# Moving a head's weight maxima and scaling between phases of a gated delta-net block on Trainium2

## The chip, the core and the metric

The kernel runs on one core of one Trainium2 chip. The core has five engines that run their own instruction streams and meet at semaphores: TensorE (PE, matrix products), VectorE (DVE), ScalarE (ACT), GpSimd (POOL) and SyncE (SP, which here only issues transfers). Transfers between the chip's memory and the engines' memory go through queues that an engine fills: SyncE, ScalarE and GpSimd each have one here. The metric is the device time of one launch in microseconds (us), the median of several runs.

## The reference

The block adds half a feed-forward branch, an attention branch and half a feed-forward branch again, each behind a layer norm, to x of 4 x 512 tokens by 512 features. The weights of the feed-forward branch (2048 inner features) are rebuilt from spline control points. The attention branch is a gated delta rule, a recurrence over tokens with a 128 x 128 state for each of 32 value heads, two to each of the 16 key heads.

```python
x = x + 0.5 * ffn(layernorm(x)); x = x + attn(layernorm(x)); x = x + 0.5 * ffn(layernorm(x))
# attn: qkvz = x @ W_qkvz (512 x 12288, 768 columns a key head); ba = x @ W_ba (512 x 64)
# q, k, v: causal convolution of 4 taps, silu; q, k: rms norm
# beta = sigmoid(b);  g = -exp(A_log) * softplus(a + dt_bias)
def step(Sst, inp):
    q_t, k_t, v_t, g_t, beta_t = inp
    Sst = Sst * jnp.exp(g_t)[..., None, None]
    kv = jnp.einsum('bhk,bhkv->bhv', k_t, Sst)
    delta = (v_t - kv) * beta_t[..., None]
    Sst = Sst + k_t[..., None] * delta[:, :, None, :]
    o = jnp.einsum('bhk,bhkv->bhv', q_t, Sst)
    return (Sst, o)
# out: rms_norm(o) * norm_w * silu(z) @ W_out
```

## The kernel before

The program is a row of phases, one behind the other: the spline phase (to about 60 us of the profiled span) rebuilds the feed-forward weights, `ffn_phase` "f1_" is the first feed-forward block (to 343), `norm_phase` (to 422) makes the second layer norm and the gates of all heads, `attn_phase` (to 3450) is the attention, and `ffn_phase` "f2_" (to the end) the second feed-forward block. Each engine has one stream of instructions per phase, in the order in which the code writes it, and instructions of one engine run in that order.

**Weights of the attention.** Products of this phase are made from 16-bit pairs. A weight is loaded as 32-bit numbers (`raw_w`, three parts of 128 x 1024 for keys and queries, values, and Z; `raw_o` for the output weight), scaled by a power of two that puts its largest entry in a fixed place, and then cast to a high and a low half on GpSimd (`split_part`, L2341 and L2342; `split_wo`, L2352 and L2353). To find the power of two, VectorE takes a maximum along each partition (`largest`, L2209), SyncE writes these to the chip's memory and reads them back to all partitions (`most_dram`, `spread`), and VectorE takes the maximum across (`power_of_two`, L1082 to L1084), makes a table of scales (`head_scales`, L1089 to L1092) and multiplies (`scale_weights`, L2228). The result's scale is undone by the table at L2202.

**The attention phase** runs 64 units j, four batches for each of 16 key heads (j // 4 is the head, j % 4 the batch). A unit first goes through the inverse steps s = 2 to 13, in which TensorE and VectorE build a triangular inverse (TensorE L1854 and L1856; VectorE's masked product L2268; ScalarE's copy L2048), with pieces of other work written between them by a dictionary `steps[s]`. Then comes the chunk phase, c = 0 to 3: the state is carried through four chunks of 128 tokens. VectorE copies or updates the state at the head of each chunk (L2286 for c = 0, L2288 for c = 1 and 2). Preparation of the next unit and output of the last one run between.

Of the next head's weights, unit 1 of a head has the maxima at steps 4, 9, 10 and 13, unit 2 the scales at step 4 and the scalings at steps 9, 9, 10 and 11:

```python
                if has_delta and j // B + 1 < NK:
                    if j % B == 1:
                        for i, s in enumerate((4, 9, 10, 13)):
                            steps[s].append(lambda i=i: largest(i))
                    if j % B == 2:
                        steps[4].append(next_scales)
                        for part, s in enumerate((9, 9, 10, 11)):
                            steps[s].append(lambda part=part: scale_weights(part))
```

GpSimd casts the new weights in units 2 and 3. SyncE's stream for a head is: decays of the next unit (`at_gb`, L1562), taps and gates of the next head (L1097 to L1099, L1568), the rows of the residual out and in (L1579, L1574), the raw parts (L1554) and the raw output weight (L1609), and later the round trip of the maxima.

**The norm phase** goes through 16 chunks of 128 tokens: statistics on VectorE (`stats`), a power on GpSimd, a scaling on ScalarE (L1326), a turn on TensorE (L1410), halves of the result on ScalarE and VectorE. The gate weights `w_ba` make a round trip of their own (maximum behind chunk 3, scales behind chunk 6 at L1082, scaling and halves on GpSimd behind chunk 7, L1231), and TensorE's first product with them, `gates_of(0)`, is L1385. The first head's raw weights are loaded (L1191), their maxima taken behind the last chunks (L1279), and the round trip ends between the two halves of the gates' work on VectorE (L1292 to L1301). The last thing of the phase is the turn of the decays on TensorE (L1416), for which L1306 on VectorE is needed.

**The first feed-forward block** starts with x turned for the first tile of 512 tokens and then runs 4 tiles t of 16 cells n. In each cell TensorE makes two products, ScalarE the SiLU (L791) and the high half (L797), VectorE the rest. Before it, on SyncE's queue, the weights are written to the chip's memory for the second block (L711, the dump: `ffn_weights<-ffn_w`).

## Time and profile before

| | |
|---|---|
| median of 3 runs | 3742.67 us (3741.57 to 3743.55) |
| the profiled execution | 3737.42 us |
| its span | 3735.7 us |
| TensorE's mean granted clock | 0.977 |

The span is the time from the first to the last instruction of the profiled execution, and all starts below count from its beginning. The profile gives the busy time of each engine (PE, DVE, ACT, POOL; PEld is TensorE's loading of weights), the order of each engine's instructions with start, length and form, and in brackets how long the engine had been idle before one and what ended that. "x3" behind a row says that three like instructions in a row are drawn together, and their time is from the start of the first to the end of the last. SPq and ACTq are issues of transfers by SyncE and ScalarE.

### The profile page before, as it was taken

Reading aid. Unit: us, or ns where it says so; the run is one execution under the profiler, and the core shown is the slowest. Engines: PE = TensorE matmul, PEld = TensorE weight load, DVE = VectorE, ACT = ScalarE, POOL = GpSimd, SP = SyncE. Lnnn points to the kernel's source line nnn. Section 1 sums busy time; section 2 is a strip of 40 time slices with the busy share of each in tenths; the row PEclk is TensorE's granted clock in tenths of the full one; section 3 lists DMA queues with packets and bytes.
Section 4 is the critical chain, followed back from the end, with each engine's and each line's share of the span. In section 5 each row is a group of like instructions: output and inputs, shape, how many; then the busy total and the mean of one; then the engine's idle time right before and its main releaser. Section 6 shows DMA issues by size and latency. Waiting matters only on the chain. (4 is left out here: it accounts for less than half of the span.)

```text
span 3735.7 us, 77363 instructions
## 1 busy us (share of the span) xinstructions
PE 3407.8 (91%) x29092; PEld 2449.2 (66%) x29092; DVE 2299.9 (62%) x4326; ACT 2091.9 (56%) x5699; POOL 2267.3 (61%) x2682
## 2 busy tenths in 40 slices
PE   5996699999999999999999999999999999996898
PEld 3884366666666666666666666666666666664687
DVE  4654566666666666666666666666666666653564
ACT  3443456665656565656566666666666665663343
POOL 2102567676767676767676767676767676763110
PEclk8998899999999999999999999999999999998999
DMA  4415111212122212121212121212121212111421
GB/s 153 127 46 86 32 62 59 83 62 80 65 77 70 72 66 75 63 79 59 83 59 83 59 83 58 83 57 83 59 84 59 83 59 83 59 68 43 167 58 35
DMA packets 211424, 272.35 MB, mean 73 GB/s; under 512 B 88944, under 2 KB 119792, under 8 KB 209904
## 3 DMA queue, kind: packets, MB, share of 16 engines
q1 hardware_dynamic: 201792, 251.50, 20.9%
q0 software_dynamic: 4464, 14.36, 1.0%
q8 instruction: 234, 3.83, 0.4%
q10 hardware_dynamic: 4800, 1.56, 0.3%
q14 instruction: 134, 1.10, 0.1%
HBM read 178.02 MB, written 89.16 MB: 72 GB/s over the span
## 5 line engine op out<-in xcount | busy, mean ns | idle before, releaser
L2048 ACT ACTIVATE at_t<-at_inv 128x512 f16<-128x512 f32 x768 | 460.6, 600 | 532.6 <-PE at_inv L1856 532.4
L2414 POOL TENSOR_TENSOR at_gm<-at_cst,at_gates 128x512 fp32r<-128x512 f32 x256 | 261.5, 1042 | 246.4 <-PE at_misc L1630 246.4
L2268 DVE TENSOR_TENSOR at_pml<-at_prod,at_cst 128x256 f16<-128x256 f32 x768 | 322.4, 420 | 132.2 <-PE at_prod L1630 122.2
L1630 PE MATMUL at_proj<-x_hi,at_w_hi 128*128 128x512 f16 x1024 | 388.6, 380 | 2.0 <-PEq L1170 2.0
L1630 PE MATMUL at_proj<-x_lo,at_w_hi 128*128 128x512 f16 x1024 | 389.2, 380 | 0.0
L1630 PE MATMUL at_proj<-x_hi,at_w_lo 128*128 128x512 f16 x1024 | 388.4, 379 | 0.0
L1854 PE MATMUL at_inv<-at_pml,at_t 128*128 128x64 f16 x3072 | 289.4, 195 | 98.7 <-DVE at_pml L2268 90.3
L1854 PEld LDWEIGHTS at_inv<-at_pml,at_t 128*128 128x128 f16 x3072 | 226.7, 98 | 221.6 <-DVE at_pml L2268 186.5
L1630 PE MATMUL at_prod<-at_t,at_nlhi 128*128 128x64 f16 (+1 forms) x3584 | 288.7, 197 | 23.9 <-DVE at_cv_z L2308 15.6
L2158 DVE SCALAR_TENSOR_TENSOR at_cv_v<-at_proj,at_cw,at_cv_v 128x511 f32<-128x511 f32 (+2 forms) x384 | 287.4, 749 | 21.8 <-ACT at_cv_v L1972 8.3
L2202 DVE SCALAR_TENSOR_TENSOR rows<-at_misc,at_tab,rows 128x512 f32<-128x512 f32 x256 | 191.2, 747 | 173.3 <-PE at_misc L1630 173.3
L1856 PE MATMUL at_inv<-at_t,at_pml 128*128 128x64 f16 x3072 | 286.4, 194 | 0.0
L1630 PE MATMUL at_proj<-at_w_hi,x_hi 128*128 128x256 f16 x1024 | 284.5, 278 | 1.6 <-DVE at_cv_q L2158 0.9
L1630 PE MATMUL at_proj<-at_w_hi,x_lo 128*128 128x256 f16 x1024 | 284.0, 277 | 0.0
L1630 PE MATMUL at_proj<-at_w_lo,x_hi 128*128 128x256 f16 x1024 | 283.7, 277 | 0.0
L915 PE MATMUL f_ring<-f_x_hi,ffn_w 128*128 128x512 f32 x640 | 247.7, 402 | 2.9 <-DVE f_x_lo L841 2.9
L1630 PEld LDWEIGHTS at_prod<-at_t,at_nlhi 128*128 128x128 f16 x3584 | 192.3, 98 | 85.4 <-issue 44.9
L2114 ACT ACTIVATE at_t<-at_inv,at_gates 128x128 f32<-128x128 f32 x512 | 159.4, 363 | 155.4 <-PE at_inv L1630 155.4
L1856 PEld LDWEIGHTS at_inv<-at_t,at_pml 128*128 128x128 f16 x3072 | 213.3, 98 | 36.2
L2288 DVE SCALAR_TENSOR_TENSOR at_t<-at_t,at_dcy,at_inv 128x128 f32<-128x128 f32 x256 | 77.6, 345 | 238.2 <-PE at_inv L1630 231.2
L1630 PE MATMUL at_misc<-at_wo_hi,at_gt_hi 128*128 128x512 f16 x512 | 198.9, 388 | 20.1 <-DVE at_gt_lo L2195 13.7
L1630 PE MATMUL at_misc<-at_wo_lo,at_gt_hi 128*128 128x512 f16 x512 | 196.2, 383 | 0.0
(323 smaller groups left out, 10160.5 us busy)
## 6 DMA issues: line engine op xcount, KB each, us to landing
rows<-x SPq DMA_DIRECT2D x64, 1024.0 KB, 5.6
x<-rows SPq DMA_DIRECT2D x64, 1024.0 KB, 4.3
at_gb<-decays SPq DMA_DIRECT2D x64, 512.0 KB, 3.7
at_raw_w<-w_qkvz SPq DMA_DIRECT2D x48, 512.0 KB, 7.7
ffn_weights<-ffn_w SPq DMA_DIRECT2D x1, 11776.0 KB, 36.6
ffn_w<-ffn_weights POOLq DMA_DIRECT2D x4, 2688.0 KB, 24.1
at_raw_o<-w_out SPq DMA_DIRECT2D x16, 512.0 KB, 3.5
f_xnext<-x_in SPq DMA_DIRECT2D x4, 1024.0 KB, 5.2
```

Of the source, the lines that this page charges most:

```text
L915: return nc.tensor.matmul(out, lhsT, rhs, start=start, stop=stop)
L1630: return nc.tensor.matmul(out, lhsT, rhs, start=start, stop=stop)
L1854: nc.tensor.matmul(half_of(ch(psT[g], c), level, 0), ch(t16[:, g, 1], c), half_of(ch(pml[:, level - 1, g], c), level, 0), start=False, sto ...
L1856: last = nc.tensor.matmul(half_of(ch(psT[g], CH + c), level, 1), ch(pml[:, level - 1, g], c), half_of(ch(t16[:, g, 1], c), level, 1), star ...
L2048: own["a_t"].up(A(grown(t16[:, s % R].rearrange("p a t -> p (a t)"), s // R), grown(psT[s % R], s // R), ACT.Copy))
L2114: own["a_d"].up(A(delta[:, h, :], ch(psY, h), ACT.Copy, scale=gcur[:, 2, at + c, h:h + 1]))
L2158: ins = V.scalar_tensor_tensor(out[:, s:S], unit_bank[u][:, 0:S - s], cw[(j + 1) // B % 2][:, u, 3 - s:4 - s], out[:, s:S], ALU.mult, ALU.add)
L2202: own["d_y"].up(V.scalar_tensor_tensor(row, out_bank[:], tab[:, of // B % 2, 7:8], row, ALU.mult, ALU.add))
L2268: own["d_p"].up(V.tensor_tensor(pml[:, level - 1, g].rearrange("p (c b a m) -> p c b a m", c=CH, a=2, m=m)[:, :, :, 0, :], psP[:, 0:S // 2 ...
L2288: ins = V.scalar_tensor_tensor(state[:, h, :], state[:, h, :], dcy[:, j % 2, h, c:c + 1], ch(psU, h), ALU.mult, ALU.add)
L2414: last = G.tensor_tensor(gm[:, k], incl.unsqueeze(1).to_broadcast([P, CH, P]), new_gates[:, g, at:at + CH, h:h + 1].to_broadcast([P, CH, P ...
```

## The change

It moves all work on weight scales out of the inverse steps and out of the norm phase.

In the attention phase a new function `weights(c)` is called at the head of each chunk, ahead of the state's copy or update. Unit 0 has three maxima in chunk 0; unit 1 the scales in chunk 0 and one scaling each in chunks 1 and 2; unit 2 the third scaling and the maximum of the output weight in chunk 0; unit 3 the scale of the output weight in chunk 0 and its scaling in chunk 1. The round trip is two now, of three maxima and of one. SyncE issues the raw parts before taps, gates and rows.

The first head's weights and the gate weights are taken in the first feed-forward block: ScalarE issues seven loads behind its second row sum, into the two `rows` buffers (free until the norm phase) and small new tiles; VectorE takes the five maxima in cells 8, 13, 14 and 15 of tile 0 and makes scales and tables in cells 14 and 15 of tile 1; SyncE does the round trip in tile 1; GpSimd casts the gate weights in tile 2. The norm phase loads the first head's parts again, as before, and VectorE multiplies each as it lands with the scales that are there already; the output weight is scaled at the phase's end. A class `FirstHead` holds the tiles and semaphores.

```diff
@@ ffn_phase, SyncE
                         sp.dma_start(xnext[:], xv[t + 1]).then_inc(xnext_in, 16)
+                    if first and t == 1:
+                        sp.wait_ge(first.largest, 5)
+                        sp.dma_start(first.largest_dram, first.most[:]).then_inc(first.stored, 16)
+                        sp.wait_ge(first.stored, 16)
+                        sp.dma_start(first_spread, first.largest_dram.rearrange("q n -> (q n)").partition_broadcast(P)).then_inc(first.back, 16)
@@ ffn_phase, ScalarE
                 for c in range(2):
                     high_xs(0, c)
+                if first:
+                    w_qkvz, w_out, w_ba_in, norm_w, bits_in = first_in
+                    for i in range(3):
+                        act.dma_start(raw[i].rearrange("p (j n) -> p j n", j=HB),
+                                      w_qkvz[:, i * PART:(i + 1) * PART].rearrange("(j p) n -> p j n", p=P)).then_inc(first.loaded, 16)
+                    act.dma_start(raw[3].rearrange("p (r n) -> p r n", r=R), w_out[0:R * D, :].rearrange("(r p) n -> p r n", p=P)).then_inc(first.loaded, 16)
+                    act.dma_start(first.nw[:], norm_w.rearrange("(p a) -> p a", a=1)).then_inc(first.loaded, 16)
+                    act.dma_start(first.exponent[:], bits_in).then_inc(first.loaded, 16)
+                    act.wait_ge(first.cleared, 1)
+                    act.dma_start(w_ba[:, :, 0:2 * NV], w_ba_in.rearrange("(j p) n -> p j n", p=P)).then_inc(first.loaded, 16)
                 for t in range(NT):
@@ ffn_phase, VectorE
+                        if first and t == 0:
+                            for i in {8: (0,), 13: (1,), 14: (2,), 15: (3, 4)}.get(n, ()):
+                                first_largest(i)
+                        if first and t == 1 and n == 14:
+                            first_scales()
+                        if first and t == 1 and n == 15:
+                            first_tables()
@@ norm_phase, VectorE
-                    if c == 3:
-                        dve.wait_ge(ba_in, 16)
-                        nc.vector.tensor_reduce(ba_most[:], w_ba[:].rearrange("p j n -> p (j n)"), mybir.AxisListType.X, ALU.max,
-                                                apply_absolute_value=True).then_inc(ba_max, 1)
...
                 for c in range(NCH - 3, NCH):
+                    part = c - NCH + 3
                     low(c)
-                    dve.wait_ge(raw_in[c - NCH + 3], 16)
-                    nc.vector.tensor_reduce(most[:, c - NCH + 3:c - NCH + 4], raw_w[:, c - NCH + 3].rearrange("p j n -> p (j n)"),
-                                            mybir.AxisListType.X, ALU.max, apply_absolute_value=True).then_inc(head_max, 1)
...
+                    dve.wait_ge(raw_in[part], 16)
+                    nc.vector.tensor_scalar(raw_w[:, part], raw_w[:, part], tab[:, 0, part:part + 1], None, ALU.mult).then_inc(head_scaled, 1)
...
-                    if i == 0:
-                        dve.wait_ge(head_back, 16)
-                        dve.wait_ge(factors_set, 2)
-                        power_of_two(nc.vector, chain, mp, spread, exponent, 4)
-                        chain(head_scales(nc.vector, chain, tab[:, 0, :], mp, rcp, factors))
-                        for part in range(3):
-                            nc.vector.tensor_scalar(raw_w[:, part], raw_w[:, part], tab[:, 0, part:part + 1], None, ALU.mult).then_inc(head_scaled, 1)
-                        nc.vector.tensor_scalar(raw_o[:], raw_o[:], tab[:, 0, 3:4], None, ALU.mult)
@@ norm_phase, TensorE
                     pe.wait_ge(xhi_done, (b + 1) * CH)
-                    if b == 0:
-                        pe.wait_ge(split, 3)
@@ attn_phase, SyncE
                 if kh + 1 < NK:
                     if kh > 0:
-                        sp.wait_ge(sems["a_d"], R * CH * first)
-                    load_gates(kh + 1)
-                next_rows(first)
-                if kh + 1 < NK:
-                    if kh > 0:
                         sp.wait_ge(sems["p_w"], 2 * kh)
                         sp.wait_ge(sems["p_z"], kh)
                     load_part(sp, kh + 1, 0, "l_kq")
                     load_part(sp, kh + 1, 1, "l_v")
                     load_part(sp, kh + 1, 2, "l_z")
+                    if kh > 0:
+                        sp.wait_ge(sems["a_d"], R * CH * first)
+                    load_gates(kh + 1)
+                next_rows(first)
+                if kh + 1 < NK:
+                    sp.wait_ge(sems["d_max_w"], 3 * (kh + 1))
+                    sp.dma_start(most_w_dram, most[:, 0:3]).then_inc(most_stored, 16)
...
@@ attn_phase, VectorE
+                def weights(c):
+
+                    if j % B == 0 and c == 0:
+                        for part in range(3):
+                            largest(part)
+                    if j % B == 1 and c == 0:
+                        scales()
+                    if j % B == 1 and c in (1, 2):
+                        scale_weights(c - 1)
+                    if j % B == 2 and c == 0:
+                        scale_weights(2)
+                        largest_out()
+                    if j % B == 3 and c == 0:
+                        scales_out()
+                    if j % B == 3 and c == 1:
+                        scale_out_weights()
...
                 for c in range(CH):
+                    if has_delta and j // B + 1 < NK:
+                        weights(c)
                     if has_delta and c < CH - 1:
```

The order on VectorE, before: the scales in the inverse steps of unit 2 of a head, between the masked products (L2268, `at_pml`).

```order
L2268 TENSOR_TENSOR at_pml<-at_prod,at_cst 128x64x4
L1082 TENSOR_REDUCE at_mp<-at_spread 128x4
L1083 TENSOR_SCALAR at_mp<-at_mp 128x4
L1084 TENSOR_TENSOR at_mp<-at_mp,at_exponent 128x4
L1089 RECIPROCAL at_rcp<-at_mp 128x4
L1090 TENSOR_TENSOR at_tab<-at_rcp,at_factors 128x4
L1091 TENSOR_TENSOR at_tab<-at_mp,at_factors 128x4
L1092 TENSOR_TENSOR at_tab<-at_tab,at_mp 128x1
L2268 TENSOR_TENSOR at_pml<-at_prod,at_cst 128x64x4
```

And after, the chunk phase of unit 1: the scales stand ahead of the state's copy (`at_t<-at_inv`, now L2352), and a scaling of a raw part (L2280) ahead of each of the two updates (now L2354).

```order
L614 TENSOR_REDUCE first_mp<-at_spread_w 128x3
L615 TENSOR_SCALAR first_mp<-first_mp 128x3
L616 TENSOR_TENSOR first_mp<-first_mp,first_exponent 128x3
L621 RECIPROCAL first_rcp<-first_mp 128x3
L622 TENSOR_TENSOR first_tab<-first_rcp,first_factors 128x3
L623 TENSOR_TENSOR first_tab<-first_mp,first_factors 128x3
L2352 COPY at_t<-at_inv 128x128 x2
...
L2280 TENSOR_SCALAR at_raw_w<-at_raw_w,first_tab 128x1024
L2354 SCALAR_TENSOR_TENSOR at_t<-at_t,at_dcy,at_inv 128x128 x2
...
L2280 TENSOR_SCALAR at_raw_w<-at_raw_w,first_tab 128x1024
L2354 SCALAR_TENSOR_TENSOR at_t<-at_t,at_dcy,at_inv 128x128 x2
```

What left the inverse steps now stands before the state's copy and updates, six instructions in place of seven.

On ScalarE, at the start of the first feed-forward block, after: the turned x (L831), the row sums (L837), the seven loads, and the first SiLU (L875; L791 before, where it followed the row sums directly).

```order
L831 ACTIVATE f_x_hi<-f_ring 128x512 x4
L837 ACTIVATE f_xs_hi<-f_ring 128x512 x2
L862 DMA rows<-w_qkvz 128x4x256 x3
L864 DMA rows<-w_out 128x2x512
L865 DMA first_nw<-norm_w 128x1
L866 DMA first_exponent<-exponent_bits 128x5
L868 DMA f_w_ba<-w_ba 128x4x64
L875 ACT_TABLE_LOAD
L875 ACTIVATE f_sg<-f_ring 128x512
```

The seven issues stand between the row sums and the SiLU; nothing else of ScalarE's stream in this block moved.

On SyncE in the attention phase, before, from the decays of a head's second unit on:

```order
L1562 DMA at_gb<-decays 128x1024
L1097 DMA at_cw_raw<-conv_w 128x4
L1098 DMA at_cw_raw<-conv_w 128x4
L1099 DMA at_cw_raw<-conv_w 128x2x4
L1568 DMA at_gates<-gates 128x160
L1579 DMA x<-rows 128x4x512
L1574 DMA rows<-x 128x4x512
L1554 DMA at_raw_w<-w_qkvz 128x4x256 x3
L1609 DMA at_raw_o<-w_out 128x2x512
```

And after, the same stretch:

```order
L1606 DMA at_gb<-decays 128x1024
L1598 DMA at_raw_w<-w_qkvz 128x4x256 x3
L1197 DMA at_cw_raw<-conv_w 128x4
L1198 DMA at_cw_raw<-conv_w 128x4
L1199 DMA at_cw_raw<-conv_w 128x2x4
L1612 DMA at_gates<-gates 128x160
L1623 DMA x<-rows 128x4x512
L1618 DMA rows<-x 128x4x512
L1653 DMA part_largest<-first_most 128x3
L1655 DMA at_spread_w<-part_largest 128x384
L1657 DMA at_raw_o<-w_out 128x2x512
```

The raw parts moved ahead of taps, gates and rows, and the round trip of their maxima follows the rows.

## Rows read from the trace of the kernel before

**Rows 1.** The page's busy times (us, share of the span, instructions) by engine

```profile
PE 3407.8 (91%) x29092; PEld 2449.2 (66%) x29092; DVE 2299.9 (62%) x4326; ACT 2091.9 (56%) x5699; POOL 2267.3 (61%) x2682
```

**Rows 2.** Timeline of VectorE, state copies: start, length, instruction, [idle before <- releaser]

```profile
477.40 0.49 DVE L2286 COPY at_t<-at_inv 128x128 f32<-128x128 f32 x2 [5.04 <-PE at_inv L1630]
...
989.61 0.49 DVE L2286 COPY at_t<-at_inv 128x128 f32<-128x128 f32 x2 [4.16 <-PE at_inv L1630]
...
1034.37 0.49 DVE L2286 COPY at_t<-at_inv 128x128 f32<-128x128 f32 x2 [4.17 <-PE at_inv L1630]
...
1080.07 0.49 DVE L2286 COPY at_t<-at_inv 128x128 f32<-128x128 f32 x2 [4.16 <-PE at_inv L1630]
...
1130.21 0.49 DVE L2286 COPY at_t<-at_inv 128x128 f32<-128x128 f32 x2 [4.16 <-PE at_inv L1630]
...
3366.50 0.49 DVE L2286 COPY at_t<-at_inv 128x128 f32<-128x128 f32 x2 [4.16 <-PE at_inv L1630]
```

**Rows 3.** Timeline of TensorE, an inverse step of unit 2 behind the scales

```profile
919.06 0.20 PE L1854 MATMUL at_inv<-at_pml,at_t 128*128 128x64 f16 x1 [2.63 <-DVE at_pml L2268]
```

**Rows 4.** Timeline of VectorE, state updates of chunks 1 and 2 behind 989.61

```profile
994.37 0.61 DVE L2288 SCALAR_TENSOR_TENSOR at_t<-at_t,at_dcy,at_inv 128x128 f32<-128x128 f32 x2 [1.92 <-PE at_inv L1630]
...
999.53 0.61 DVE L2288 SCALAR_TENSOR_TENSOR at_t<-at_t,at_dcy,at_inv 128x128 f32<-128x128 f32 x2 [1.76 <-PE at_inv L1630]
```

**Rows 5.** The tile at_raw_w: ns min/median/max, first and last start us; landing of loads

```profile
L2209 DVE TENSOR_REDUCE at_most<-at_raw_w x45: 1207/1210/1211, 498.3 to 3124.4; 128x1 f32<-128x1024 f32 x45
L2228 DVE TENSOR_SCALAR at_raw_w<-at_raw_w,at_tab x45: 745/1407/1749, 558.4 to 3174.9; 128x1024 f32<-128x1024 f32 x45
...
DMA to landing us min/median/max: 5.0/7.7/10.1
```

**Rows 6.** Timeline of SyncE's issues in unit 0 of a head

```profile
1019.69 0.33 SPq L1562 DMA_DIRECT2D at_gb<-decays  x1
```

**Rows 7.** Timeline of GpSimd: half of a split, and the key norms' first step

```profile
935.04 0.75 POOL L2335 TENSOR_SCALAR at_cw<-at_cw_raw,at_tab 128x8 f32<-128x8 f32 x1
...
936.43 1.15 POOL L2342 TENSOR_TENSOR at_w_lo<-at_raw_w,at_w_hi 128x512 f16<-128x512 f32 x1
...
982.96 0.23 POOL L2420 TENSOR_SCALAR at_rr<-at_ss 128x4 f32<-128x4 f32 x1 [1.65 <-issue]
```

**Rows 8.** Timeline of VectorE and TensorE in the norm phase

```profile
365.28 0.28 DVE L1082 TENSOR_REDUCE nm_ba_tab<-nm_ba_spread 128x1 f32<-128x128 f32 x1 [7.70 <-DMA nm_ba_spread<-ba_largest]
...
372.11 0.59 PE L1385 MATMUL nm_baT<-x_hi,nm_ba_hi 128*128 128x512 f16 x1 [11.81 <-POOL nm_ba_lo L1231]
...
416.13 2.05 PE L1416 MATMUL nm_turn<-nm_expo,at_cst 128*128 128x512 f32 x2 [18.31 <-DVE nm_expo L1306]
```

**Rows 9.** Start of block f1: issues, the SiLU, dump's landing, 70 to 76 us

```profile
76.93 0.51 SPq L711 DMA_DIRECT2D ffn_weights<-ffn_w  x1
...
85.20 0.60 ACT L791 ACTIVATE f_sg<-f_ring 128x512 f32<-128x512 f32 x1
...
ffn_weights<-ffn_w SPq DMA_DIRECT2D x1, 11776.0 KB, 36.6
...
70.00:76.00 6.00, 3.67 (x16) 3.13 (x16) 3.75 (x9) 1.83 (x4) 0.87 (x1) 0.50 0.00 0
```

The page's line gives size and time from issue to landing. The last line's columns are window, sum, then busy time (count) of PE, PEld, DVE, ACT, POOL, TensorE's granted clock, the transfers' share and GB/s.

**Rows 10.** Transfers by queue, packets, MB, share: two of 3470:3485, one of 85:110

```profile
q0 software_dynamic: 294, 5.63, 90.1%
q1 hardware_dynamic: 272, 0.56, 11.3%
...
q1 hardware_dynamic: 228, 10.74, 99.4%
```

The queue q0 is GpSimd's, q1 SyncE's, q10 (below) ScalarE's.

**Rows 11.** Issues by SyncE (block f2) and ScalarE (end of f1), q10 until 340.83

```profile
3468.98 18.10 SPq L686 DMA_DIRECT2D f_xres<-x  x1
...
335.35 5.49 ACTq L815 DMA_DIRECT2D x<-f_xres  x8
...
q10 hardware_dynamic: 2205, 0.27, 66.4%
```

More of the change, by code:

```diff
@@ L2218, in next_scales, with scales, scales_out @@
+                def scales():
+                    new = j // B + 1
+                    wait(dve, "l_most_w", 16 * new)
+                    chain(power_of_two(V, chain, mp[:, 0:3], spread_w[:], exponent))
+                    own["d_tab"].up(part_scales(V, chain, tab[:, new % 2, :], mp, rcp, factors))
+                    wait(dve, "d_tab", own["d_tab"].n)
+                def scales_out():
                     new = j // B + 1
-                    wait(dve, "l_most", 16 * (new + 1))
-                    power_of_two(V, chain, mp, spread, exponent, 4)
```

231 lines of the change are left out of this document (120 added, 111 removed).

## The prediction

> **What bounds the kernel now.** I read the page's head first: TensorE is busy for 91% of the span and every other engine for under two thirds [rows 1], so work moved off the path that TensorE waits on is worth its whole length, and work moved onto it costs its whole length. The share says nothing about where TensorE waits, so the second view is the order of time on VectorE. The state copy (L2286) runs once in each of the 64 units of the attention phase, at the start of the chunk phase, and its starts are a ruler. From 989.61 to 1034.37 us is one plain unit: 44.76 us. The next interval holds the inverse steps with the maxima: 45.70. The one after holds the scales and the scaling: 50.14 [rows 2]. From the first start, 477.40, to the 63rd, 3366.50, are 2889.10 us in 62 intervals; at 44.75 each they would take 2774.5. So the weight work costs 2889.1 - 2774.5 = **114.6 us** over 15 heads, 7.6 each. How it costs: while VectorE makes the scales, TensorE stands 2.63 us before the next inverse product, released by VectorE's masked product [rows 3]; the inverse steps are a ring TensorE, VectorE, TensorE, ScalarE with no slack.
>
> In the chunk phase the ring runs TensorE, ScalarE, TensorE, and VectorE joins once per chunk. It stands idle before the state updates: 4.16 us in chunk 0, 1.92 in chunk 1, 1.76 in chunk 2 of a plain unit, each ended by TensorE [rows 2, 4].
>
> **Part 1: the attention phase.** Each head's work now lies ahead of a state update. Durations and landing times are in [rows 5].
> - Unit 0, chunk 0: three maxima at 1.21 = 3.6 us in a 4.16 us gap. The data must be there: a weight load takes 5.0 to 10.1 us to land. The loads are now issued before the gates and the row traffic, right behind the decay load, whose issue begins at 1019.69 in such a unit [rows 6]. Behind it (0.33) and at 0.5 us an issue the last is out by 1021.5 and lands between 1026.5 and 1031.6; the gap runs from 1030.2 to 1034.37.
> - Unit 1, chunk 0: six small operations. The reduction shrinks from 512 to 384 elements. I take 3.4 us at most. Chunks 1 and 2: one scaling each, 0.75 to 1.75 us, median 1.41, in 1.92 and 1.76 us.
> - Unit 2, chunk 0: one scaling and one maximum, 2.9 us in 4.16. Unit 3: about 2.3 us of small operations in chunk 0 and a scaling of 1.4 in 1.92.
>
> All fit, so I take the 114.6 us as gone on VectorE, with 0 to 0.4 us left over per gap. What is late next is GpSimd in unit 2. There the first half of the new weights is split between the query's SiLU and the key norms. Before, this hid behind VectorE's stall. The half, with the tap scaling ahead of it, takes 935.04 to 937.58, 2.5 us of which I put 0.4 down to contention. In a plain unit GpSimd idles 1.65 us before the key norms [rows 7]. Of 2.1 to 2.5 us, 1.65 are covered: 0.4 to 0.9 are exposed at most. I take 0.4 x 15 = 6, since GpSimd had nothing to wait for in that idle time (its cause is its own issue) and the norms may have a little slack. Sum: **-108**, from -113 to -98 with a worse fit in chunk 2. Beside the same row, the Trainium skill (SBUF — State Buffer, "SBUF: two separate sides") says that VectorE's two-port operations and GpSimd exclude each other for a whole instruction; the spread 0.75 to 1.75 of the same scaling agrees. Were every gap to meet a busy GpSimd, the longest scaling would still be 1.75 against 1.76 and 1.92.
>
> **Part 2: the norm phase.** The gate weights' round trip goes: VectorE stood 7.70 us for it, and TensorE's first gate product waited 11.81 us, until 372.11, for the split. It was ready for it at 360.3, and nothing else is missing then, so the product now starts 11.8 us earlier. The head's round trip goes too; it stood on the way to the decays, for which TensorE waited 18.31 us, until 416.13 [rows 8]. With maxima, tables and the wait gone, VectorE reaches the gates about 13 us earlier; but its work on them will still meet GpSimd's weight split, which now comes at the same time. I carry the decays from 416.1 to 394: **-22**, between -15 and -26.
>
> **Part 3: the first feed-forward block.** This is where the change adds. VectorE gets five maxima (4 x 1.21 by [rows 5], and 0.6 for the gate weights of half the size) and a dozen small operations in cells 8 and 13 to 15 of tile 0 and 14, 15 of tile 1. VectorE is busy for only 62% of the span [rows 1] and its waits would take up most of it; fully exposed, the maxima of one cell and its neighbours are some 4 us. I take 1.5 us, 0 to 4.
>
> The seven loads on ScalarE's queue are the other matter. They stand ahead of the first SiLU (85.20), and issuing alone is 7 x 0.5 = 3.5 us. SyncE has just issued the weight dump, 11.8 MB, at 76.93; it lands 36.6 us later, at 113.5 [rows 9]. Three rows decide. (a) The dump moves in large packets: 228 packets of 47 KB in 25 us [rows 10], 9.1 per us over 16 engines. (b) Where two queues compete, packets alternate: in 3470 to 3485, in the last block, GpSimd's queue moved 294 packets (5.63 MB) and SyncE's 272 (0.56 MB) [rows 10]. (c) An issue blocks its engine when too much is queued: there SyncE's third small load took 18.10 us to issue, until the big transfer was through. ScalarE's eight stores at the end of the block, 512 packets each, took 5.49 us to issue, and 2205 packets had been moved when the last was issued: 4096 - 2205 = 1891 queued [rows 11]. The new loads make 3 x 512 (1 KB rows) + 256 + 128 + 128 + 512 = 2560 packets. To issue the last, about 2560 - 1891 = 670 must be through; while the dump runs, at most 27 us x 9.1 = 250 get through. So ScalarE stands at the seventh load (or the sixth) until the dump is done, near 113, and about 1.5 us more for the rest, at 1 KB packets. The SiLU starts at about 114.5 in place of 85.2: +29. TensorE, which has three banks, stops. When it began again after the last pause, its granted clock was 0.50, the lower level of 1.2 GHz, over all of 70 to 76 us [rows 9]; 5 us of work at half speed cost 2.5 us more. VectorE's first maximum then comes 29 us later, long after the loads have landed. Sum of part 3: 29 + 2.5 + 1.5 = **+33**, bounds below.
>
> The Trainium skill (DMA: Bandwidth & Descriptors, "Queues, rings and completion order") says that a DMA engine drains 9 to 17 descriptors of one ring before it turns to the next. By that rule the 160 small ones per engine would pass in about ten turns, and the queue would not fill for long. The trace's one for one (294 against 272) speaks against it, if its packets are descriptors; the rule's result is rival B.
>
> **The sum.** Profiled run: span 3735.7, and 3737.4 with what lies around it, 5.3 below the median of 3742.67. -108 - 22 + 33 = -97. Span 3639, median 3742.67 - 97 = **3646**.
>
> **The rivals.** A difference of 0.2%, 7.5 us, is what a measurement of this kernel can tell from none.
> - A, as above: 3646, own range 3633 to 3661. Chance 0.53.
> - B, ScalarE isn't blocked for long. It pays 3.5 us of issue; a cell takes at most (335.35 - 85.20) / 64 = 3.9 us [rows 9, 11], so VectorE comes to cell 8 between 115 and 120, and if the loads still trail the dump it waits up to 5 us: with 1.5 for the maxima some 10 us. -108 - 22 + 10: 3623. If the loads drain early too, 3619. Chance 0.24. Against it: the 18.10 us issue.
> - C, the gaps don't hold all of it: loads land late in unit 0, or GpSimd, locked out by scalings, hands on its products late. At 3 us a head it is 45 us more: 3691. Chance 0.13. Against it: 0.5 to 1.3 us of spare in each gap's sum.
> - D, slower: the state update is the node of the chunk ring, and each operation queued ahead of it delays it in full, since VectorE can't start them early (its wait for the Z unit or for a landed load ends late). The work is 3.6 + 3.4 + 4 x 1.4 + 1.4 + 2.3 = 16.3 us a head, x 15 = 244. Against 114.6 saved: 3742.7 + 130 - 22 + 33 = 3884. It turns slower when over 40% of the work is exposed (6.5 us a head). Against it: the gap is idle from VectorE's last operation on. Chance 0.04.
> - E, the norm phase keeps its length since the second half's loads or the split bound it, with all else as in A: 3668. Chance 0.06.
>
> **How the numbers follow.** The range takes A with its bounds, E, most of B, and leaves out D and most of C: 3615 to 3672. A, B, E and C hold 0.96 and all end faster by over 0.2%; I give 0.02 of it to a C twice its price, within 0.2%. So faster 0.94, within 0.2% 0.02, slower 0.04 (D).
>
> **What would show it.** In the profile after: state copies 44.75 us apart, 45.2 in each fourth; VectorE's idle before them under 1 us in units 0 and 1. One issue on ScalarE's queue near 86 us that lasts over 20 us, with TensorE idle beside it (A); or none over 2 us, and VectorE waiting for the loads at its first maximum (B). The first gate product about 12 us after the turns begin and not 22. State copies 2 or more us further apart would make C, 16 us a head D.

## The result and the profile after

The changed kernel takes **3643.31 us** (median of 4 runs, 3642.28 to 3643.93) against 3743.11 for the kernel before (4 runs): a ratio of 0.973, 95% interval 0.972 to 0.975. The forecast was 3646. The profiled execution has a span of 3641.8 us, against 3735.7 before.

The head of the page after, with busy time by engine (compare [rows 1]):

```profile
span 3641.8 us, 77463 instructions
...
PE 3397.8 (93%) x29092; PEld 2448.0 (67%) x29092; DVE 2282.5 (63%) x4402; ACT 2090.7 (57%) x5699; POOL 2268.9 (62%) x2680
```

The busy times hardly moved. What moved is where VectorE's work stands. Here are the state copies (now L2352) at the start of the chunk phases of units 11 to 15, which answer to [rows 2]; 1029.15 is a unit with the three maxima, 1073.96 one with the scales.

```profile
984.45 0.49 DVE L2352 COPY at_t<-at_inv 128x128 f32<-128x128 f32 x2 [2.54 <-issue]
...
1029.15 0.49 DVE L2352 COPY at_t<-at_inv 128x128 f32<-128x128 f32 x2 [0.78 <-PE at_inv L1677]
...
1073.96 0.49 DVE L2352 COPY at_t<-at_inv 128x128 f32<-128x128 f32 x2 [2.44 <-issue]
...
1118.91 0.49 DVE L2352 COPY at_t<-at_inv 128x128 f32<-128x128 f32 x2 [1.83 <-PE at_inv L1677]
...
1163.73 0.49 DVE L2352 COPY at_t<-at_inv 128x128 f32<-128x128 f32 x2 [2.54 <-issue]
```

All four intervals are near the plain unit of 44.76: 44.70, 44.81, 44.95 and 44.82. The 50 us interval is gone, and so is the 45.7. The idle time before the copy, 4.16 us in the kernel before, is 0.78 behind the three maxima, and 1.83 behind a scaling and a maximum. "issue" with 2.4 to 2.5 us stands where scales were made just before: the engine went through its own short chain.

In the first feed-forward block, ScalarE's timeline (ACTq are its issues of transfers):

```profile
85.06 0.60 ACT L837 ACTIVATE f_xs_hi<-f_ring 128x512 fp32r<-128x512 f32 x1 [2.20 <-PE f_ring L1033]
85.07 2.27 ACTq L862 DMA_DIRECT2D rows<-w_qkvz  x3
87.37 24.94 ACTq L864 DMA_DIRECT2D rows<-w_out  x1
112.34 0.93 ACTq L865 DMA_DIRECT2D first_nw<-norm_w  x1
113.29 1.30 ACTq L866 DMA_DIRECT2D first_exponent<-exponent_bits  x1
114.63 0.45 ACTq L868 DMA_DIRECT2D f_w_ba<-w_ba  x1
115.11 1.28 ACT L875 ACT_TABLE_LOAD   x1 [29.45 <-issue]
116.40 0.60 ACT L875 ACTIVATE f_sg<-f_ring 128x512 f32<-128x512 f32 x1
```

One issue, of the fourth load, holds ScalarE for 24.94 us, and the first SiLU starts at 116.40 in place of 85.20 [rows 9]. TensorE stops with it: its next product, at 117.05, was 28.19 us idle. Transfers by queue in 87.37 to 112.31:

```profile
q1 hardware_dynamic: 223, 10.50, 97.4%
q10 hardware_dynamic: 207, 0.21, 2.4%
```

SyncE's dump moved 223 packets of 47 KB and ScalarE's queue 207 of 1 KB: one for one again, as in [rows 10]. The order of the packets shows it in small steps too: from 89.20 to 91.05 us, about the time of one 47 KB packet (1.74 us), the two queues moved 16 packets each, as many as there are transfer engines.

The places that cut the program into phases, in both profiles (us from the span's start; the last two columns are lengths):

| | first SiLU | last stores of f1 | state copy 1 | state copy 63 | span | copies 1 to 63 | behind copy 63 |
|---|---|---|---|---|---|---|---|
| before | 85.20 | 335.35 | 477.40 | 3366.50 | 3735.7 | 2889.10 | 369.2 |
| after | 116.40 | 367.80 | 491.38 | 3270.21 | 3641.8 | 2778.83 | 371.6 |
| difference | +31.2 | +32.45 | +13.98 | -96.3 | -93.9 | -110.3 | +2.4 |

So by profiles the first block costs 32.5 us, the stretch from its last stores to the first copy gives 18.5, the attention gives 110.3, and the end 2.4 more. That is 93.9 us between two profiled executions; between medians it is 99.8, mainly since the profiled execution of the kernel before was 5.3 us below its median. Against a second profile of the kernel before (below, "The kernel before once more") the same four are 30.1, 20.5, 105.4, and 0.7 less in place of 2.4 more.

### The profile page after: what moved, and what is told of

It reads as the page before. It is cut to its first block and busy times, and to the rows that moved or that the text cites. A ratio compares the mean times of both kernels' runs of the same rounds, so it can differ in the third digit from the quotient of the medians.

```text
span 3641.8 us, 77463 instructions
## 1 busy us (share of the span) xinstructions
PE 3397.8 (93%) x29092; PEld 2448.0 (67%) x29092; DVE 2282.5 (63%) x4402; ACT 2090.7 (57%) x5699; POOL 2268.9 (62%) x2680
## 5 line engine op out<-in xcount | busy, mean ns | idle before, releaser
L1901 PE MATMUL at_inv<-at_pml,at_t 128*128 128x64 f16 x3072 | 286.1, 194 | 11.8 <-DVE at_pml L2332 1.1
L2249 DVE SCALAR_TENSOR_TENSOR rows<-at_misc,first_tab,rows 128x512 f32<-128x512 f32 x256 | 191.1, 747 | 164.2 <-PE at_misc L1677 164.2
L2354 DVE SCALAR_TENSOR_TENSOR at_t<-at_t,at_dcy,at_inv 128x128 f32<-128x128 f32 x256 | 77.6, 345 | 197.2 <-PE at_inv L1677 189.0
```

Of the source, the lines that this page charges most:

```text
L1901: nc.tensor.matmul(half_of(ch(psT[g], c), level, 0), ch(t16[:, g, 1], c), half_of(ch(pml[:, level - 1, g], c), level, 0), start=False, sto ...
L2249: own["d_y"].up(V.scalar_tensor_tensor(row, out_bank[:], tab[:, of // B % 2, 7:8], row, ALU.mult, ALU.add))
L2354: ins = V.scalar_tensor_tensor(state[:, h, :], state[:, h, :], dcy[:, j % 2, h, c:c + 1], ch(psU, h), ALU.mult, ALU.add)
```

## The experiments

The theory on trial: (1) the attention's gain is that of the place, and it holds only as long as work and data fit the idle time before a state update; (2) the first block's loss is ScalarE's blocked issue, caused by the dump. The rivals are with each expectation. Times are medians of 4 or 5 executions; the two runs on the order of the loads and the kernel before once more are single executions, without an interval. Each ratio is to the kernel before on the same chip. Its median there was 3739.5 us beside the attention part alone, the later dump, the early loads and the loads on SyncE's queue behind the dump; 3742.8 beside the inverse steps, the raw loads behind the rows, the two more maxima and the narrow loads first; 3736.5 beside the loads ahead of the dump, the wide load first and the kernel before once more. The changed kernel had 3743.1 beside it, so differences of a few us between it and an experiment can be the chip's.

### The attention part alone

The kernel of before, with the change's code for the attention phase (weights at the chunks' heads, two round trips, raw loads first) and nothing else of it.

> The kernel of before with the attention part of the change alone; the first feed-forward block and the norm phase are as before. Theory (the parts add up: attention -110.3 by the state copies, first block +33.3, norm phase -19.3): 3743.1 - 110 = 3633. Rival (part of the attention's gain comes from tables and tiles that the first part moved): over 3640. It should be faster than the whole change by 10 to 14 us.

Measured: **3633.27 us** (ratio 0.972, 0.970 to 0.973); copies 1 to 63 take 2779.62, within 0.8 of the whole change's. So the attention part doesn't need the other two. Together those cost more than they give. The medians differ by 10.0 us, but the gains over the kernel before beside each are 106.3 and 99.8, 6.5 apart, and the intervals of the two ratios overlap. The two profiles show where it goes: in the changed kernel the first SiLU is 30.2 us later, the cells take 1.2 more, and the stretch from the last stores to the first copy is 18.9 shorter; the spans differ by 10.9.

### The weight work back in the inverse steps

```diff
-                    if has_delta and j // B + 1 < NK:
-                        weights(c)
...
+                if has_delta and j // B + 1 < NK:
+                    if j % B == 1:
+                        for part, s in enumerate((4, 9, 10)):
+                            steps[s].append(lambda part=part: largest(part))
+                    if j % B == 2:
+                        steps[4].append(scales)
+                        for part, s in enumerate((9, 9, 10)):
+                            steps[s].append(lambda part=part: scale_weights(part))
+                        steps[13].append(largest_out)
+                    if j % B == 3:
+                        steps[9].append(scales_out)
+                        steps[11].append(scale_out_weights)
```

> The changed kernel, but the attention's weight work stands in inverse steps again: three maxima in unit 1 (steps 4, 9, 10), scales in unit 2 (step 4), three scalings (9, 9, 10), the output weight's maximum at 13, and its scale and scaling in unit 3 (9, 11). The two round trips and SyncE's order are those of the change. Theory (the place is what gives the gain): the 110 us come back, 3753, slower than the kernel of before by 0.3%; with the scale work split over two units it may cost 10 us more. Rival (the split into two round trips, or SyncE's order, gave part of it): 3700 or less.

Measured: **3770.98 us** (ratio 1.007, 1.006 to 1.009), and 2907.05 from copy 1 to 63, which is 128.2 more than in the changed kernel. The mean intervals that end with the copies of a head's units 1, 2, 3 and 0 are 45.38, 50.45, 47.24 and 44.76 us: unit 3, plain before, now pays 2.5 for the output weight's scale and scaling. The expectation, 3753, had named 10 us on top as possible for the split; 18 came. The place gives the gain; two round trips in the old place cost 18 us more than one between copies 1 and 63 (2907.05 against 2889.10).

### The raw loads behind the rows

```diff
                 if kh + 1 < NK:
-                    if kh > 0:
-                        sp.wait_ge(sems["p_w"], 2 * kh)
-                        sp.wait_ge(sems["p_z"], kh)
-                    load_part(sp, kh + 1, 0, "l_kq")
...
                 next_rows(first)
                 if kh + 1 < NK:
+                    if kh > 0:
+                        sp.wait_ge(sems["p_w"], 2 * kh)
+                        sp.wait_ge(sems["p_z"], kh)
+                    load_part(sp, kh + 1, 0, "l_kq")
```

> The changed kernel, but SyncE issues the three raw parts behind taps, gates and rows, where they stood before. Theory (the maxima in unit 0 fit only because the loads were moved forward): the issues start at 1029.7 in the unit whose copy stood at 1034.4, the last part lands 5 to 10 us behind its issue at 1031, near 1039, the third maximum ends near 1040, and the state copy is 5 us late in each fourth unit: 15 x 5.3 = 80, 3723. Rival (landing is not on the path): 3643.

Measured: **3769.07 us** (ratio 1.006, 1.005 to 1.008): slower than the kernel before. Timeline of VectorE in such a unit, then SyncE's issue:

```profile
1046.69 1.22 DVE L608 TENSOR_REDUCE first_most<-at_raw_w 128x1 f32<-128x1024 f32 x1 [6.02 <-DMA at_raw_w<-w_qkvz]
1048.16 1.22 DVE L608 TENSOR_REDUCE first_most<-at_raw_w 128x1 f32<-128x1024 f32 x1 [0.25 <-DMA at_raw_w<-w_qkvz]
1051.03 1.22 DVE L608 TENSOR_REDUCE first_most<-at_raw_w 128x1 f32<-128x1024 f32 x1 [1.65 <-DMA at_raw_w<-w_qkvz]
1052.16 0.48 DVE L2352 COPY at_t<-at_inv 128x128 f32<-128x128 f32 x2
...
1040.13 2.15 SPq L1598 DMA_DIRECT2D at_raw_w<-w_qkvz  x3
```

The mechanism is the expected one, and it costs half as much again as the 80 us expected: 120.0 us more than in the changed kernel between copies 1 and 63, 8.0 a head. The interval with the wait is 51.27 us on average, 6.6 too long, where 5.3 was expected: the loads are issued behind the 1 MB of rows (1039.66) and share the transfer engines with it. The next interval is 46.26, 1.4 too long. TensorE had stood for 6.77 us, and its granted clock in the six microseconds behind is 0.69 where it is 1.00 in the same place of the changed kernel (1029.60 to 1035.60): the 1.4 us are read as the price of that clock; no run separated them from other causes.

```profile
1052.60:1058.60 6.00, 5.89 (x27) 4.34 (x28) 2.52 (x5) 2.50 (x6) 1.13 (x2) 0.69 0.29 33
```

This is rival C of the prediction, made real, at 8.0 us a head and not 3: the three maxima go free only with SyncE's new order. In the changed kernel the three run in one go, 1024.90 to 1028.36, without a wait.

### Two more maxima in unit 0

```diff
                         for part in range(3):
                             largest(part)
+                        for part in range(2):
+                            chain(largest_of(V, most[:, 4:5], raw_w[:, part].rearrange("p j n -> p (j n)")))
```

> The changed kernel with two more maxima of 128 x 1024 (unused results) behind the three in unit 0, chunk 0. VectorE was idle for 0.78 us before the copy there. Theory (what doesn't fit in the idle time is paid in full, since the state is on the ring): 2.42 - 0.78 = 1.64 us a head and some 0.1 for the links, 15 x 1.7 = 25: 3668. Rival (later slack takes it up): under 3650. Rival (nothing was hidden, each operation costs its length): 15 x 2.5 = 38, 3681.

Measured: **3663.29 us**, 20.0 above the changed kernel. The interval that ends with the late copy is 46.33 us in place of 44.70: +1.63, and 2.42 - 0.78 = 1.64 was the part that doesn't fit. The next interval is mostly 44.53 and not 44.81, so 0.28 comes back. 15 x 1.35 = 20.3. The theory holds with the small correction: an operation at the chunk's head is free up to the idle time there and costs nearly its length behind it, as rival D had it for all of the work.

### The dump after the loads

```diff
                     if t == 0 and w_known:
+                        sp.wait_ge(first.loaded, 16 * 7)
                         sp.dma_start(w_dram, wts[:].bitcast(F32)).then_inc(w_stored, 16)
```

> The changed kernel, but SyncE issues the weight dump only when ScalarE's seven loads have landed. Theory (the loads' packets take turns with the dump's large ones, ScalarE's queue fills, and the issue of the fourth load blocks for 24.94 us): with an empty transfer system no issue lasts over 2 us, the first SiLU starts near 90 us and not at 116.4, and the kernel takes 3643.3 - 26 = 3617. Rival (the queue fills by the loads' own number, 2560 packets, whatever else runs): the fourth issue still blocks, if shorter, and the time stays over 3635. Rival (the dump, now beside the first cells, costs as much as it gives): 3640.

Measured: **3614.78 us** (ratio 0.967, 0.965 to 0.968), 28.5 below the changed kernel (25 by the gains over the kernel before beside each), and 18.5 below the attention part alone, beside the same kernel before. So with this wait the two other parts of the change pay. The first SiLU is 28.1 us earlier than in the changed kernel, of which 1.9 stood ahead of the loads already (first row sum at 80.38 and 82.26). ScalarE's timeline:

```profile
83.19 1.50 ACTq L863 DMA_DIRECT2D rows<-w_qkvz  x3
84.72 0.53 ACTq L865 DMA_DIRECT2D rows<-w_out  x1
85.28 0.78 ACTq L866 DMA_DIRECT2D first_nw<-norm_w  x1
86.09 0.45 ACTq L867 DMA_DIRECT2D first_exponent<-exponent_bits  x1
86.58 0.44 ACTq L869 DMA_DIRECT2D f_w_ba<-w_ba  x1
87.06 1.28 ACT L876 ACT_TABLE_LOAD   x1 [3.28 <-issue]
88.35 0.60 ACT L876 ACTIVATE f_sg<-f_ring 128x512 f32<-128x512 f32 x1
```

The same seven issues take 3.9 us, none over 1.5. Both rivals are out: the number of packets alone doesn't block, and the dump, issued at 93.51, costs next to nothing beside the cells (first SiLU to last stores 250.96, and 250.13 in the next run with the same later dump, against 250.15 in the kernel before and 251.40 in the changed one).

### The loads earlier, or on SyncE's queue

The dump as late as in the last run, and the loads moved ahead of ScalarE's row sums:

> As the kernel with the later dump, and the seven loads are issued between ScalarE's turned x and its row sums, where it was idle for 5.33 us. Theory: the 3.5 us of issues are covered as well; first SiLU near 86 us, time 3643.3 - 31 = 3612, 5 below the kernel with the later dump alone. Rival (the loads, at the start of the block, delay the x and residual loads or the row sums): the same as that kernel or above, 3617 or more.

Measured: **3610.82 us** (ratio 0.965, 0.964 to 0.967). Better by 4.0, against 5 expected. The cover was not whole: one of the issues took 3.31 us, and the row sums began at 84.58, where they stood at 80.38 with the dump later alone; the first SiLU is at 87.83. That is only 0.5 us earlier than with the later dump alone (88.35). TensorE's granted clock over 76 to 82 us, ahead of it, was 0.50 in this profile and 0.96 in that one, which may hide part of what the cover gives. Of the 3.8 us between the two spans 0.8 are in the cells, 0.5 in the attention and 1.9 behind copy 63, where nothing was changed. So the total near the forecast doesn't show that the cover gave 4 us.

Then, the changed kernel with the loads issued by SyncE, behind the dump in its queue:

> The changed kernel, but the seven loads are issued by SyncE behind the dump. ScalarE then issues nothing. Theory: the first SiLU is back at 85 to 86 us; the loads land some 8 us behind the dump, near 123, while VectorE comes to its first maximum near 113, and waits there about 10 us with TensorE behind it: 3643.3 - 31 + 10 = 3622. Rival (TensorE's cost was not ScalarE's blocked issue but the transfers themselves): no change, 3643. Rival (buffers between the engines hide the 10 us): 3612.

Measured: **3620.99 us** (ratio 0.968, 0.967 to 0.970). ScalarE is free (first SiLU 86.31), and the blocked issue moves to SyncE, which has nothing else to do there; VectorE pays at its first maximum. The first row is SyncE's, the second VectorE's:

```profile
78.56 28.03 SPq L775 DMA_DIRECT2D rows<-w_qkvz  x3
...
121.59 1.22 DVE L608 TENSOR_REDUCE first_most<-rows 128x1 f32<-128x1024 f32 x1 [8.41 <-DMA f_w_ba<-w_ba]
```

From the first SiLU to the last stores are 259.69 us, 8.3 more than in the changed kernel: the wait of 8.41 is paid in full. This is near rival B's sum in the prediction (3623), and for its reason, late loads at VectorE's first maximum, though SyncE issued them.

Last, SyncE issues them directly ahead of the dump:

> The changed kernel, but SyncE issues the seven loads, directly ahead of the weight dump in the same queue, and ScalarE none. Theory: SyncE has nothing else to do there, so the dump starts some 4 us later and no engine pays; the loads land near 88 us, long before VectorE's first maximum near 113. First SiLU between 85 and 86.5; against the kernel with ScalarE's early loads (first SiLU 87.83, 3610.8) 1 to 2 us better: 3609. Rival (the loads, behind the x and residual loads of the first tiles, still delay what the first cells need): 3613 or more.

Measured: **3612.39 us** (ratio 0.967, 0.965 to 0.968). A miss by 3 us: not better than ScalarE's early loads. The first SiLU is at 87.17 and not by 86.5, as the second row sum began at 85.20. Beside that stands TensorE's granted clock at the block's start: 0.55 over 76 to 82 us in this run (below, second row) and 0.59 in the changed kernel's (first row), where it is 0.96 in the first profile of the kernel before (first row sum at 80.43) and 0.50 in its second (82.84).

```profile
76.00:82.00 6.00, 4.59 (x14) 3.44 (x13) 1.38 (x2) 0.64 (x2) 0.00 (x0) 0.59 0.66 232
...
76.00:82.00 6.00, 4.59 (x13) 3.52 (x13) 1.36 (x2) 0.60 (x1) 0.00 (x0) 0.55 0.71 253
```

The clock differs from run to run of one kernel, so the loads need not be its cause. But the clock doesn't explain the miss against the early loads: the first SiLU is 0.7 us earlier than theirs, the cells take the same 250.1 us, and what is longer by profile is the end behind copy 63, 373.19 against 371.27, which no run here explains. The three kernels that take the loads out of the dump's way lie within 4 us of each other; all are faster than both the kernel before and the changed one.

### How full the queue gets: the order of the seven loads

Narrow loads first, then the raw parts, then the output weight:

> The changed kernel with the four small or narrow loads in another order: norm weight (128 packets), exponent bits (128), gate weights (512), then the three raw parts (512 each) and the output weight (256). Sums behind each: 128, 256, 768, 1280, 1792, 2304, 2560. In the changed kernel the issue that brought the sum from 1536 to 1792 blocked. Theory (the queue holds some 1600 packets): the issue of the second raw part, which brings it to 1792, blocks until the dump is through. Rival (it holds a number of transfers, three): the first raw part's issue blocks. Rival (it holds 1891 or more, as at the end of the block): the third raw part's does. The time stays within 5 us of 3643 in all three.

Measured: 3645.36 us (one execution). The first two raw parts are issued in 1.61 us together; the third ends the group at 111.57:

```profile
86.80 1.61 ACTq L866 DMA_DIRECT2D rows<-w_qkvz  x2
...
86.80 24.77 ACTq L866 DMA_DIRECT2D rows<-w_qkvz  x3
```

So 1792 packets went in, none over 1 KB, and my 1600 fell; it was rival 1891 that came true. But then the changed kernel's fourth load, which also brings the sum to 1792, should have passed. It differs by its rows of 2 KB. Hence the wide load first:

> The changed kernel with the output weight's load (256 packets of 2 KB) ahead of the three raw parts (512 of 1 KB each), then the small ones. Sums: 256, 768, 1280, 1792, then 1920, 2048, 2560. With 1 KB packets a sum of 1792 had passed, with the wide load last it had blocked. Theory (the 2 KB rows take two places each in the queue): the third raw part brings the places to 2048 and blocks. Rival (places are packets, and what blocked was another thing): the third raw part passes in 1 us, and a later load blocks. The time is 3643 within 5 us either way.

Measured: 3638.72 us (one execution). The wide load and two raw parts pass, and the third raw part, which brings the packets to 1792 again, blocks:

```profile
86.76 21.82 ACTq L863 DMA_DIRECT2D rows<-w_qkvz  x1
```

With rows of at most 1 KB 1792 packets pass; with 256 of 2 KB among them 1792 don't, first or last. If each 2 KB row takes two places, the three orders agree with a limit between 1792 and 2048. A limit in bytes would fit the three as well (1536 KB pass twice, 1667 block once), but SyncE's queue took the dump of 11.8 MB in one issue of 0.51 us [rows 9]; no run tests it on ScalarE's. How full the queue is when a blocked issue returns gives no single number. In the changed kernel 207 packets had been moved then, so 2048 - 207 = 1841 places were taken, beside the 1891 of [rows 11]. With the wide load first the 175 moved were its 2 KB rows (0.36 MB), 350 places by this theory, which leaves 1698; with the narrow loads first it is 2304 - 207 = 2097. So two places for a 2 KB row is a reading that foretold which load would block; what the limit is, and when a blocked issue goes on, stays open.

### The kernel before once more

> The kernel of before once more, for a second profile. The first had a span of 3735.7 and ran at 3737.42, 5.3 below the median of its runs. Theory: one run of this kernel differs from another by the starts of phases (the load of constants at the last block's start, TensorE's clock there), not by its units: from the first to the 63rd state copy again 2889.1 within 1, and the rest spread over the phases. Rival: the units themselves differ from run to run, 2892 or more.

Measured: 3740.03 us (one execution), span 3738.3. Neither the theory nor the rival: copies 1 to 63 take 2884.21 us, 4.9 **less** than in the first profile, while the first SiLU is at 87.62 and not at 85.20, the first copy at 481.83 and not at 477.40, and the stretch behind copy 63 has 372.26 and not 369.20. The difference in the attention is in the interval with the scaling, 51.05 us on average and 51.38 in the first profile; the other three are equal within 0.01. Units do differ from run to run then, where VectorE's scalings stand in the inverse steps. A phase's length from one profile is good to some 3 to 5 us, and the attention's gain is 104 to 110 by these profiles.

## Why the prediction was right

**Attention.** Predicted -108, measured -110.3 (-105.4 against the second profile). The inverse steps without the work and the chunk phases with it are both as forecast; the run with the work back in the inverse steps shows that the place is the cause. Each gap held its work as the steps said: three maxima left 0.78 us of 4.16 (0.5 predicted), a scaling and a maximum left 1.83 (1.3 predicted). The scalings in chunks 1 and 2 left 0.99 and 0.87 us:

```profile
897.44 0.96 DVE L2280 TENSOR_SCALAR at_raw_w<-at_raw_w,first_tab 128x1024 f32<-128x1024 f32 x1
899.39 0.60 DVE L2354 SCALAR_TENSOR_TENSOR at_t<-at_t,at_dcy,at_inv 128x128 f32<-128x128 f32 x2 [0.99 <-PE at_inv L1677]
...
902.70 0.97 DVE L2280 TENSOR_SCALAR at_raw_w<-at_raw_w,first_tab 128x1024 f32<-128x1024 f32 x1
904.55 0.61 DVE L2354 SCALAR_TENSOR_TENSOR at_t<-at_t,at_dcy,at_inv 128x128 f32<-128x128 f32 x2 [0.87 <-PE at_inv L1677]
```

One takes 0.96 us here, where the median in the inverse steps was 1.41 [rows 5]; over all heads it is 0.95 to 1.29 us. What was next late was GpSimd's half split in unit 2, as predicted; its timeline there, then the same instruction in the plain unit behind:

```profile
932.02 1.16 POOL L2408 TENSOR_TENSOR at_w_lo<-at_raw_w,at_w_hi 128x512 f16<-128x512 f32 x1
933.25 0.23 POOL L2485 TENSOR_SCALAR at_rr<-at_ss 128x4 f32<-128x4 f32 x1
...
977.75 0.23 POOL L2485 TENSOR_SCALAR at_rr<-at_ss 128x4 f32<-128x4 f32 x1 [1.68 <-issue]
```

The idle 1.68 us are gone in unit 2, and the interval that ends with its copy is 44.95 in place of 44.76: 0.19 us a head where 0.4 was taken, 3 us and not 6 over 15. No experiment separated it from the scalings in the same interval, so its share is read, not shown.

**Norm phase.** Predicted -22 by the decays, measured -21.6 there: their turn stood 80.78 us behind the last stores of the block and now stands 59.17 behind (426.97 - 367.80). The two steps held as well. The first gate product comes 10.49 us behind the start of the turns and no longer 22.51, so 12.0 sooner (11.8 predicted), and from it to the decays are 32.74 us in place of 44.02. At the first state copy only 18.5 are left. The step that failed is the silent one, that what is behind the decays only shifts. The stretch behind them, in us:

| | stores to decays | decays to first product | first product to copy 1 | the first product's length |
|---|---|---|---|---|
| before | 80.78 | 6.65 | 54.62 | 0.38 |
| before, once more | 81.13 | 6.63 | 56.34 | 0.38 |
| after | 59.17 | 7.24 | 57.17 | 0.59 |
| narrow loads first | 59.71 | 7.25 | 57.10 | 0.58 |
| raw loads behind the rows | 59.04 | 7.25 | 56.34 | 0.38 |
| early loads | 57.27 | 7.24 | 56.35 | 0.38 |
| wide load first | 57.02 | 7.23 | 56.37 | 0.38 |

Of the missing 3.1 us, 0.6 lie between the decays and the attention's first product, in every kernel with the new norm phase (TensorE idles 2.64 us there where it idled 2.03). The other 2.55 lie behind that product, and 1.7 of them are what two profiles of the kernel before differ by. The last 0.8 go with TensorE's clock. Where the first product takes 0.59 or 0.58 us, the granted clock is at the lower level (1.2 GHz); first row after, second row before:

```profile
433.00:439.00 6.00, 4.79 (x12) 1.79 (x13) 0.00 (x0) 0.00 (x0) 4.83 (x3) 0.50 0.84 249
...
422.00:428.00 6.00, 5.22 (x24) 2.28 (x24) 1.65 (x3) 0.69 (x1) 5.26 (x3) 1.00 0.86 258
```

12 products in place of 24 in the same time, and yet the first copy comes only 0.8 us later than in the other changed kernels of the table, whose first product takes 0.38: the rest doesn't reach it. The norm phase up to the decays differs by some 2 us between kernels with the same code there (59.0 to 59.7 and 57.0 to 57.3 above); its cause stays open.

**First block.** Predicted +33, measured +32.45. Its terms: the SiLU was to be 29.3 later and was 31.2 later, of which 1.8 stood ahead of the loads already (the row sum at 85.06 and not at 83.23), as it did in other runs, the kernel before's second profile among them. The block itself, from the row sum's start to the SiLU, grew by 31.34 - 1.97 = 29.4. Clock and VectorE were to cost 2.5 + 1.5 and cost 1.25 together (251.40 - 250.15). After the stop the clock was 0.50, as foreseen (115 to 121 us); and with the loads ahead of the dump, where the maxima are the same, the stretch is 250.15, so VectorE's work in the cells costs nothing, and the 1.25 are left for the stop. Without the 1.8 us of a late start the block costs 30.6, so +33 against +32.45 is in part luck.

Which load blocks was predicted as the seventh or sixth and was the fourth. The limit taken, 1891 packets, is near what the changed kernel shows if the wide load takes 512 places (1841); why it blocked there is a reading, as said above. It changed nothing in the sum. In all three orders the seven loads were out only when the dump was nearly through: at 115.1 in the changed kernel, 114.3 with the narrow loads first and 115.1 with the wide load first, where a second issue stood for 4.63 us.

The one for one of the packets held. By the rule of the Trainium skill (DMA: Bandwidth & Descriptors, "Queues, rings and completion order") a DMA engine drains 9 to 17 descriptors of one ring before it turns to the next. By an estimate from that page's figure and this trace's packet, each engine would then have moved at least 9 packets of the dump in a row, 9 x 1.74 = 15.7 us. The trace has 16 packets of each queue from 89.20 to 91.05 us. If packets are descriptors, the rule doesn't hold here. The prediction also drew the wrong thing from it. The dump's queue would have had such turns too, and its 256 packets are 16 for an engine, one or two turns, so by the rule as well ScalarE's loads would have stood behind most of the dump; rival B was not its result.

**The sum.** -110.3 - 18.5 + 32.45 + 2.4 = -93.9 between profiles; -99.8 between medians. The forecast was -97. Part of the closeness is luck. The attention came out 2.3 us better than forecast, and clock and VectorE in the first block 2.8 better; the first SiLU was 1.9 worse, the stretch before the first copy 3.5 and the end, forecast to stay, 2.4. These partly cancel, and a phase's length from a single profile is uncertain by as much.

## What to carry to other kernels

Find the instruction that the ring waits for, read the idle time in front of it, and put side work there up to that length and no further: 3.5 us of work in a gap of 4.16 was free, and 1.6 us beyond it cost 1.6; but check that its data has landed by then, since the loads, issued some 5 us ahead of the gap's end and not 14, turned the attention's gain of 110 us into a loss of 10, by profiles. Before adding small loads to a queue of a compute engine, look what large transfer is under way at that time: their packets take turns one for one, and a full queue stops the engine itself. A change that helps as a whole can hold a part that loses: here the parts outside the attention cost some 6 to 11 us net, and one wait on another queue turned that into a gain of 18.5 over the attention part alone.

## What was unexpected of the hardware

- An issue of a small load stood for 24.94 us and stopped ScalarE, while its packets of 1 KB and SyncE's of 47 KB took turns one for one (16 and 16 in 1.85 us, 207 and 223 in all).
- 1792 packets passed into ScalarE's queue with rows of at most 1 KB, and blocked with 256 rows of 2 KB among them, in either order. That a 2 KB row takes two places is a reading, not shown.
- A stop of 6.77 us on TensorE was followed by a granted clock of 0.69, and the following unit was 1.4 us longer.
- The scaling of 128 x 1024 elements took 0.95 to 1.29 us in the chunk phase, where it took 0.75 to 1.75, with a median of 1.41, in the inverse steps [rows 5].
- TensorE's clock at the start of a phase, behind a pause, was the lower level in one run and the full one in another of the same kernel (0.96 and 0.50 over 76 to 82 us), with a first SiLU 2.4 us later. At the start of the attention the same difference moved the first copy by only 0.8 us.
